# Moving GpSimd's token scatters behind other steps of the attention pipeline

## The reference, cut to what matters

```python
x = L0_attn_x                       # 8 x 1024 tokens of 128 features, float32
xn = _layernorm(x, axis=-1)
x = x + linear_attn(xn, W_qkv, W_o) + ffn(xn, ...)

# linear_attn: 16 heads of 8, chunks of 64 tokens, a state S carried over the chunks
inter = jnp.einsum('bhde,bthe->bthd', S, q_c)
scores = jnp.where(causal, jnp.einsum('bthd,bshd->bhts', q_c, k_c), 0.0)
intra = jnp.einsum('bhts,bshd->bthd', scores, v_c)
S = S + jnp.einsum('bthd,bthe->bhde', v_c, k_c)

# ffn: each token goes to the one of 8 experts with the highest affinity
assign = jnp.argmax(x @ centroids.T, axis=1)
xhat = (x - mu) * jax.lax.rsqrt(var + LN_EPS)
h = relu(einsum('etd,efd->etf', xhat * ln_g + ln_b, w1) + b1)   # 512 wide
y = x + einsum('etf,edf->etd', h, w2) + b2
gated = a * y + (1 - a) * x         # a = sigmoid(x @ centroids.T); the row of the chosen expert is kept
```

## Time and profile before

| | before |
|---|---|
| median of 3 runs | 364.52 us (364.34 to 366.64) |
| span of the profiled execution | 363.3 us |
| PE busy | 342.1 us (94%) |
| DVE busy | 287.1 us (79%) |
| ACT busy | 241.8 us (67%) |
| POOL busy | 251.7 us (69%) |
| 64 scatters to `slots_d` (L420) | 64.2 us, 1003 ns each |
| 71 scatters to the output (L494) | 112.9 us, 1590 ns each |

### The profile page before, as it was taken

One profiled execution on the slowest core, in us unless ns is written; L12 is line 12 of the kernel. 1 busy time (PEld: TensorE's weight loads), 2 busy tenths in 40 slices (PEclk: granted clock), 3 DMA queues, 4 the chain that ended last, 5 costly groups with the idle time before them and its releaser, 6 DMA issues.

```text
span 363.3 us, 17565 instructions
## 1 busy us (share of the span) xinstructions
PE 342.1 (94%) x6868; PEld 293.0 (81%) x6868; DVE 287.1 (79%) x799; ACT 241.8 (67%) x657; POOL 251.7 (69%) x245
## 2 busy tenths in 40 slices
PE   6799999998999999999999989999999999999991
PEld 6466786776787687777867879999999999999990
DVE  8888897898886888878877786788777788777860
ACT  4788687677587666757566735766666667666660
POOL 3488477789788765556455513888888888888884
PEclk9989999999999999999999999999999999999996
DMA  6220433636314021545553445555545555555420
GB/s 196 70 60 8 118 91 97 184 104 194 106 47 120 19 87 54 157 109 163 150 152 93 131 105 134 72 73 72 72 65 74 71 63 74 74 76 59 38 23 0
DMA packets 55153, 33.18 MB, mean 91 GB/s; under 512 B 5352, under 2 KB 52768, under 8 KB 55072
## 3 DMA queue, kind: packets, MB, share of 16 engines
q1 hardware_dynamic: 42800, 23.53, 23.9%
q0 software_dynamic: 12272, 8.54, 17.2%
HBM read 18.72 MB, written 13.78 MB: 89 GB/s over the span
## 4 chain that ended last, share of the span: by engine, by line
issue 25%; POOL 13%; PE 11%; DVE 1%; DMA 1%; POOLq 1%; ACT 1%; SPq 0%; DVEq 0%; ACTq 0%
POOL out_dram L494 13%; PE bank L1328 2%; PE sc L1274 2%; PE bank L1337 2%; PE bank L1222 1%; DMA out_dram<-res 1%; POOLq L71 1%; PE bank L1200 1%; PE bank L1306 1%; DVE pr L856 1%; PE bank L1209 1%; PE bank L1295 1%; PE bank L1255 1%; PE bank L1215 0%; PE bank L1233 0%
## 5 line engine op out<-in xcount | busy, mean ns | idle before, releaser
L494 POOL DMA_INDIRECT out_dram<-qx,rows x71 | 112.9, 1590 | 35.1 <-issue 22.1
L694 ACT ACTIVATE qx<-sc,b1T 128x128 f32<-128x128 f32 x280 | 79.8, 368 | 39.6 <-PE sc L1421 39.6
L420 POOL DMA_INDIRECT slots_d<-rows,pos_i x64 | 64.2, 1003 | 43.1 <-issue 11.0
L856 DVE TENSOR_TENSOR pr<-sc,causal 128x1536 f32<-128x1536 f32 (+2 forms) x33 | 63.6, 1929 | 17.4 <-PE sc L1274 17.2
L1429 PE MATMUL bank<-tokens,qx 128*128 128x128 f32 x568 | 75.3, 276 | 0.8 <-ACT qx L694 0.7
L1421 PE MATMUL sc<-wide,tokens 128*128 128x128 f32 x560 | 74.0, 275 | 0.2 <-issue 0.2
L1429 PEld LDWEIGHTS bank<-tokens,qx 128*128 128x128 f32 x568 | 69.0, 192 | 1.4 <-ACT qx L694 1.4
L1421 PEld LDWEIGHTS sc<-wide,tokens 128*128 128x128 f32 x560 | 68.1, 192 | 0.3 <-issue 0.3
L1015 DVE COPY tokens<-xT 128x1024 f32 x71 | 55.2, 778 | 0.0
L1274 PEld LDWEIGHTS sc<-qx,kT 32*64 32x64 f32 x2048 | 32.5, 132 | 16.4 <-issue 15.8
L1030 DVE SCALAR_TENSOR_TENSOR qx<-bank,rows,qx 128x128 f32<-128x128 f32 x71 | 24.9, 350 | 26.3 <-PE bank L1429 25.8
(11 more groups left out here) (167 smaller groups left out, 532.2 us busy)
## 6 DMA issues: line engine op xcount, KB each, us to landing
rows<-slots_d SPq DMA_DIRECT2D x71, 66.0 KB, 2.0
res<-in_L_attn_x_dram SPq DMA_DIRECT2D x16, 256.0 KB, 4.1
out_dram<-res SPq DMA_DIRECT2D x16, 256.0 KB, 3.4
tokens<-in_L_attn_x_dram SPq DMA_DIRECT2D x7, 512.0 KB, 4.2
w1raw<-in_L_ffn_w_dram SPq DMA_DIRECT2D x8, 256.0 KB, 4.0
w2raw<-in_L_ffn_w_dram SPq DMA_DIRECT2D x8, 256.0 KB, 4.3
out_dram<-qx,rows POOLq DMA_INDIRECT x71, 3.4
slots_d<-rows,pos_i POOLq DMA_INDIRECT x64
```

The source lines that it names most:

```text
L420: pool.indirect_dma_start(slots_d, bass.IndirectOffsetOnAxis(ap=pos_i[:, t:t + 1], axis=0), rows[:, t, :], None, bounds_check=E * RT * P - ...
L494: pool.indirect_dma_start(out_rows, bass.IndirectOffsetOnAxis(ap=xs[:, a, D + 2:D + 3].bitcast(U32), axis=0), ye[:, a, :], None, bounds_ch ...
L694: last = nc.scalar.activation(ht[:, k % 2, c * P:(c + 1) * P], inner(k)[:, c * P:(c + 1) * P], ACT.Relu, bias=b1T[:, bass.ds(e * FC + c, 1)])
L856: nc.vector.tensor_tensor(pr[:, h % 2, a:G, w].rearrange("p g (j t) -> p g j t", t=CH), sc[:, a * BANK:G * BANK].rearrange("p (g w) -> p g ...
```

## The change

It changes only which semaphore GpSimd waits for before its scatters, and how many follow each wait. In quads 7 and 8 (odd half) three scatters instead of two stand at the end. From quad 9 on each quad had seven scatters, each behind a wait of its own; now it has six: two behind the weights' transposes of the quad before (`w2_ps`), two behind the state step (`ds_ps`), one behind the odd half's scores (`sc_ps`) and one behind the next quad's values (`v_ps`).

```diff
@@ -464,25 +464,21 @@
                     if n + 1 < LATE:
                         values_own(n + 1)
                     if n >= 3:
-                        send_rows(2)
+                        send_rows(3 if n + 1 >= NCH else 2)
             for h in range(ROUTED, NH):
                 n = h // 2
 
-                pool.wait_ge(s("sc_ps"), h + 1)
-                send_rows(1)
                 if h % 2 == 0:
-                    pool.wait_ge(s("av_ps"), h)
+                    pool.wait_ge(s("w2_ps"), n - 7)
+                    send_rows(2)
+                    pool.wait_ge(s("ds_ps"), n + 1)
+                    send_rows(2)
+                else:
+                    pool.wait_ge(s("sc_ps"), h + 1)
                     send_rows(1)
                     if n + 1 < NQ:
-                        pool.wait_ge(s("q_ps"), n + 2)
+                        pool.wait_ge(s("v_ps"), n + 2)
                         send_rows(1)
-                elif n + 1 < NQ:
-                    pool.wait_ge(s("v_ps"), n + 2)
-                    send_rows(1)
-                    pool.wait_ge(s("out_ps"), n)
-                    send_rows(1)
-                    pool.wait_ge(s("w2_ps"), n - 6)
-                    send_rows(1)
             assert sent[0] == NT
```

## The result

| | before | changed |
|---|---|---|
| median of all runs | 365.45 us (8 runs) | 368.47 us (8 runs) |
| ratio of the runs | | 1.0077, 95% interval 1.0051 to 1.0104 |
| span of the profiled execution | 363.3 us | 367.2 us |

The changed kernel is 0.8% slower, 2.8 us by the ratio (1.9 to 3.8). That is under the 1% that was called "no change", but clear of zero. The profiled span grew by 3.9 us, more than the ratio says, so single terms are read from the profile and the size of the whole from the ratios. One profile is one execution: the changed kernel's took 368.92 us, 0.45 above the median of its runs.

The account below looks back on a forecast made before the run. The expert stage has a fixed length, so the attention stage and the passage through SP's queue decide. Terms 0 (fewer scatters) + 0 (third scatter) + 3.6 (late last scatter) us on 364.5 gave 368.1 us, range 366.2 to 369.6.

Parts of the forecast that it names:

- the forecast case: At the passage to the experts, the late last scatter delays SP's reads: +3.6 us, range 367.3 to 369.0, chance 0.44.
- Fewer scatters at other places: Late quads from quad 9: 43 scatters become 41 at other places, cost 0, range -1.0 to +0.5 us.
- VectorE's shared port: Rival: scatter pairs behind the state step slow VectorE's two-input state additions, 2 us on top, 370.1 us; chance 0.04.
- TensorE's gaps: Rival: fewer scatters close TensorE's idle before weight loads, quads 9 to 15; half is 4.3 us, 363.8; chance 0.06.
- The third scatter: Quads 7 and 8: 1.3 us of GpSimd ahead of half 16's mask, 1.5 us of cover left, cost 0.
- The last scatter: GpSimd's 64th scatter waits for the scores of half 31 and starts at 214.0 instead of 210.00, 4.0 us later.
- Its landing in 2.2 us: The last scatter lands in 2.2 us instead of 3.1, so SP passes at 216.2 instead of 213.1, +3.1 us.
- The held read: Instruction fetch holds SP's first or second read, not the seventh, for 1.50 us; second tile scaled 3.6 us later.
- The stores: SP's stores leave 3.1 us later and land at 226.1, before the first result at about 226.6 needs them.
- The four ahead: Quad 15's four scatters ahead of the last are no obstacle; the pair behind the state step runs about 210.5 to 213.0.
- 1.2 us lie outside the span: Premise: profiled span 363.3 us against a median of 364.52; the forecast difference is added to the median.
- The rival that the early reads aren't held: Second read goes out 0.55 us after the first; gates shift 2.0 to 3.1 us, time 366.5 to 367.6; chance 0.30.

Follow-up runs that it names:

- the last scatter alone: Kernel before with only the 64th scatter moved, to wait for the scores of half 31 instead of half 30; ratio 1.0102.
- the third alone: Kernel before with nothing but a third scatter in quads 7 and 8; ratio 1.0019.
- the gates first: Kernel before with the third scatter in quads 7 and 8, and ScalarE's first eight gates ahead of the last quad's copy and first ReLU; ratio 1.0028.
- the early scatter: Changed kernel with a third scatter behind the weights' transposes in quads 12 to 14, leaving two for quad 15; ratio to the kernel before 0.9985.
- 22 dummies: Changed kernel with 22 unused transposes on TensorE between the products of half 31 and the first tile's transpose; ratio to the kernel before 1.0085.
- the later one: Changed kernel with the 64th scatter behind the products of half 30 instead of the scores of half 31; ratio to the kernel before 1.0141.
- the later one with dummies: Changed kernel with the 64th scatter behind the products of half 30, plus 30 unused transposes where TensorE idled; ratio to the kernel before 1.0098.
- the wait undone: Changed kernel whose 64th scatter follows its predecessor behind quad 15's state step, without waiting for half 31's scores; ratio to the kernel before 1.0095.

## Why the prediction was right, point by point

The time lay in the range (368.5 against 368.1 us), and the forecast case happened, step by step. That the two medians agree within 0.4 us is partly luck: the median of before rose from 364.52 (3 runs) to 365.45 (8 runs), and against it the change costs 3.0 us, by the ratio 2.8, where 3.6 was forecast. The 3.6 lies inside the ratio's interval.

- **Fewer scatters at other places: 0.** Right. From the first scores of quad 9 to the scores of half 31 the profiles have, with the places of before, 80.6, 81.1, 81.1 and 82.5 us (the kernel before, the last scatter alone, the third alone, the gates first), and with those of the change 81.9, 79.9, 81.0, 81.7, 80.8 and 80.9 (the changed one, the early scatter, 22 dummies, the later one, the later one with dummies, the wait undone). The means are 81.3 and 81.0, and single profiles of one group lie 2 us apart, so an effect under some 1 us isn't excluded. The rivals on VectorE's shared port (2 us) and on TensorE's gaps (4.3 us and more) fell with that.
- **The third scatter: 0.** Right. The changed kernel's rows for the earlier trace rows:

```profile
121.97 0.97 POOL L420 DMA_INDIRECT slots_d<-rows,pos_i  x1 [0.31 <-issue]
123.00 1.33 POOL L412 TENSOR_TENSOR pr<-pr,causal 128x512 f32<-128x512 f32 x1
...
125.50 1.12 PE L1324 MATMUL bank<-pr,vz 128*32 128x64 f32 x64
```

  The mask ends at 124.33 and is used at 125.50; 1.2 us of cover are left of the 1.5. In time the third scatter alone leaves -0.2 to +1.6 us, so the 0 rests on the profiles.
- **The last scatter: +4.0 us.** Measured 4.2 (214.21), behind scores that ended 0.2 later.
- **Its landing in 2.2 us.** Measured 2.4, so that SP passes 3.5 us later and not 3.1. It was 3.1 before.
- **The held read.** Right in place (the second) and too large: 1.00 us and not 1.50. It landed 2.46 us after its issue, and the second tile was scaled 3.5 us later, where 3.6 was forecast. The two misses cancel, which is luck. The stores, put at 226.1, had landed by 225.4 and were no obstacle, as forecast.
- **What was missing: the clock.** The prediction carried 3.6 us from the tile's scaling to the gates unchanged. In the profile they come 4.2 later, because the output and the first up-multiplication ran partly at 0.50. The ratio is smaller than that, and one thing on record goes with it: the changed kernel's eight runs go from 366.44 us at a mean clock of 0.995 to 370.51 at 0.979, and its profiled run stood at 0.988. So its runs may differ in how long the clock was low; only one of the eight has a profile, and in the six runs of the later kernel (0.979 to 0.990) the time doesn't go with the clock, so this is an indication and no more. The kernel before had a low stretch of the same length near its start, but that cost nothing that can be seen: the first scores of quad 9 start at 130.1 to 131.4 us in the five profiles with it and at 130.2 to 131.0 in the five without. The clock by 40 slices of the span on the two pages, first before, then after:

```profile
PEclk9989999999999999999999999999999999999996
```

```profile
PEclk9999999999999999999999998999999999999996
```
- **A description that fell short.** The last scatter's wait was called "the term that counts". That is true of the 64th scatter's time, but the queue of five would have brought most of the loss without the wait (ratio 1.0095 with the wait undone). The four ahead were called no obstacle, which held only because the wait came later still.

One premise was off without harm: "1.2 us lie outside the span". The changed kernel's runs each stand 1.7 to 1.8 us above their own span; the forecast added a difference to the median, so that this falls out.

The rival that the early reads aren't held went wrong in the changed kernel, where the second was held. In the later kernel its case came true: the first two reads took 0.36 and 0.35 us. The Trainium skill, "Runtime: NRT & Kernel Launch", section "Instruction fetch mechanics", calls the cost of crossing an instruction block mostly hidden. The traces agree in part: most of SP's issues beside a packet of the instruction queue took their usual time, and some took far longer, as this read with 1.00 us. That the fetch is the cause was not isolated; it rests on coincidence, told below.

## What to carry to other kernels

When a queue's last item releases the next stage, its time counts and the spacing of all others may be free: find the last landing that the next stage waits for, and how much earlier than needed it is. Moving items later by "one fewer per round" piles them up at the end, where removing the new wait alone doesn't help; count what is left for the last round. TensorE then idled for 2.9 to 3.6 us, and in three of three profiles its clock was halved around its return, so a stall can cost more than its own length.

## What the runs showed of the hardware that was not expected

**SP's DMA issues beside fetches of instructions.** In the ten profiles, all 52 DMA issues of SP between 100 and 340 us that took over 0.7 us (0.33 is usual, the longest 2.23) started between 0.20 us before and 0.58 us after the start of a 16 KB packet on the instruction queue. The reverse doesn't hold: 142 other issues of the 1100 fell into the same interval about a packet and took 0.67 us at most. So no long issue was seen without a packet, and most packets hold no issue; what sets the two kinds apart is open. The issue's duration in the changed kernel, then the DMA view of 217.5 to 218.5:

```profile
217.93 1.00 SPq L330 DMA_DIRECT2D rows<-slots_d  x1
```

```profile
q8 instruction: 1, 0.02, 5.9%
```

**The same indirect DMA landed in 2.3 to 3.7 us.** Two of the longer ones (210.00 in the kernel before, 3.1; 208.25 in the one with the early scatter, 3.7) flew while the last residual's 256 KB were being loaded; those sent at 213.7 to 215.2, after a pause of GpSimd, had nothing beside them and took 2.3 to 2.5. The load isn't the whole cause: the fifth scatter of the kernel with the wait undone took 3.0 with only the scatter before it under way, and two that flew beside a 256 KB store (the third alone, the gates first) took 2.7. So a scatter sent earlier need not land as much sooner. Measured from the start of the scores of half 31, the early scatter left 0.4 us sooner than the one of before (2.4 us ahead of them against 2.0) and let SP pass 0.2 us later (1.2 us behind against 1.1).
